# A graph layer's scatter-sum, hidden layer and normalization: batches turned in their own step, late x multiplied early, spans of 112 columns

## What is computed

```python
agg = segment_sum(edge_attr, dst, num_segments=6250)
h = concatenate([x, agg, u[batch]], axis=1)      # 128 + 128 + 16; batch is all zeros
h = relu(h @ W1 + b1)                            # 256 hidden
y = x + (h @ W2 + b2 + x)
out = (y - mean(y)) / sqrt(var(y) + 1e-5)        # over the 128 features
```

## Time and profile before

| | |
|---|---|
| Time, three runs | 185.32, 185.44, 185.79 us |
| The profiled execution: its time, its span | 185.73 us, 184.0 us |
| Granted clock of TensorE, mean | 0.994 of full speed (2.4 GHz) |
| Busy: TensorE, VectorE, ScalarE, GpSimd | 154.1, 115.4, 51.5, 25.4 us |
| DMA | 62.07 MB, mean 337 GB/s |
| HBM read and written | 58.50 MB, 3.20 MB |

### The profile page before, as it was taken

One profiled execution on the slowest core, in us unless ns is written; L12 is line 12 of the kernel. 1 busy time (PEld: TensorE's weight loads), 2 busy tenths in 40 slices (PEclk: granted clock), 3 DMA queues, 4 the chain that ended last, 5 costly groups with the idle time before them and its releaser, 6 DMA issues.

```text
span 184.0 us, 5378 instructions
## 1 busy us (share of the span) xinstructions
PE 154.1 (84%) x2195; PEld 113.9 (62%) x2195; DVE 115.4 (63%) x369; ACT 51.5 (28%) x110; POOL 25.4 (14%) x29
## 2 busy tenths in 40 slices
PE   0056979979979979969979999899889799899970
PEld 0046855955955956845846858467458568677850
DVE  6847499568376385485495466954933745877371
ACT  2021233223323313313313343133133241233230
POOL 7800030110200200200200204002003230000000
PEclk9999999999999999999999999999999999999997
DMA  5999999999999999999999999999999999998011
GB/s 119 315 352 373 374 375 373 371 373 374 374 374 373 375 372 373 376 372 373 374 373 374 375 373 374 375 373 360 363 374 374 371 374 370 367 398 303 11 43 33
DMA packets 42196, 62.07 MB, mean 337 GB/s; under 512 B 1975, under 2 KB 39541, under 8 KB 42170
## 3 DMA queue, kind: packets, MB, share of 16 engines
q1 hardware_dynamic: 41046, 61.23, 95.0%
q10 hardware_dynamic: 1124, 0.48, 1.2%
HBM read 58.50 MB, written 3.20 MB: 335 GB/s over the span
## 4 chain that ended last, share of the span: by engine, by line
PE 44%; DMA 39%; SPq 8%; DVE 4%; ACT 1%; issue 1%; DVEq 0%
DMA edge_ring<-in_edge_attr_dram 37%; PE sum_ps L845 17%; PE turn_ps L867 7%; PE hid_ps L907 6%; PE hid_ps L900 6%; PE out_ps L920 5%; SPq L276 4%; SPq L291 3%; DMA base_row<-in_dst_dram 2%; DVE bases L568 2%; PE xt_ps L920 1%; PE xt_ps L882 1%; DVE local_rows L576 1%; ACT local_t L429 1%; PE xt_ps L834 1%
## 5 line engine op out<-in xcount | busy, mean ns | idle before, releaser
L845 PE MATMUL sum_ps<-edge_ring,onehot 128*32 128x128 f32 x1662 | 58.5, 284 | 13.0 <-DMA edge_ring<-in_edge_attr_dram 10.8
L845 PEld LDWEIGHTS sum_ps<-edge_ring,onehot 128*32 128x32 f32 x1662 | 45.2, 113 | 27.9 <-DMA edge_ring<-in_edge_attr_dram 13.3
L630 DVE TENSOR_TENSOR agg_t<-agg_t,turn_ps 128x128 f32 x70 | 20.2, 288 | 56.7 <-PE turn_ps L867 52.6
L594 DVE TENSOR_TENSOR onehot<-iota,local_t 128x768 f32<-128x768 f32 (+1 forms) x40 | 33.6, 843 | 3.0 <-ACT local_t L429 2.4
L402 POOL TENSOR_TENSOR x_all<-x_all,half_b 128x512 f32<-128x512 f32 (+3 forms) x16 | 17.7, 1115 | 127.4 <-PE xt_ps L882 127.4
L466 ACT ACTIVATE hid_t<-hid_ps,bias 128x512 f32<-128x512 f32 (+3 forms) x32 | 18.1, 584 | 37.1 <-PE hid_ps L907 37.1
L867 PE MATMUL turn_ps<-place,sums 128*128 128x128 f32 (+1 forms) x140 | 26.5, 306 | 0.0
L907 PE MATMUL hid_ps<-agg_t,w_a 128*128 128x512 f32 (+3 forms) x64 | 24.1, 500 | 0.6 <-DVE agg_t L630 0.5
L867 PEld LDWEIGHTS turn_ps<-place,sums 128*128 128x128 f32 (+1 forms) x140 | 18.9, 192 | 8.0 <-issue 7.9
L920 PE MATMUL out_ps<-w_sb,hid_t 128*128 128x128 f32 (+1 forms) x176 | 21.9, 275 | 0.0
L441 ACT COPY sums<-sum_ps 128x256 f32<-128x256 f32 (+2 forms) x40 | 13.6, 341 | 25.9 <-PE sum_ps L845 25.9
(11 more groups left out here) (64 smaller groups left out, 73.0 us busy)
## 6 DMA issues: line engine op xcount, KB each, us to landing
edge_ring<-in_edge_attr_dram SPq DMA_DIRECT2D x69, 768.0 KB, 12.1
x_all<-in_x_dram SPq DMA_DIRECT2D x10, 256.0 KB, 10.5
out_dram<-x_all SPq DMA_DIRECT2D x1, 2304.0 KB
dst_rows<-in_dst_dram SPq DMA_DIRECT2D x1, 384.0 KB
x_all<-in_x_dram SPq DMA_DIRECT2D x1, 384.0 KB, 11.1
out_dram<-x_all SPq DMA_DIRECT2D x3, 128.0 KB
out_dram<-x_all SPq DMA_DIRECT2D x1, 256.0 KB
w_x<-in_L_gnn_W_dram ACTq DMA_DIRECT2D x1, 128.0 KB, 5.9
```

The lines of the kernel that those rows point to most:

```text
L594: nc.vector.tensor_tensor(onehot[0:ROWS, b % BUFFERS, 0:k * TILES], cols, loc, ALU.is_equal).then_inc(onehot_ready, 1)
L630: nc.vector.tensor_tensor(to, to, turn_ps[b % 2][:, i * SPAN:(i + 1) * SPAN], ALU.add).then_inc(group_added, 1)
L845: last = nc.tensor.matmul(bank[c * WIN:(c + 1) * WIN], onehot[0:p, b % BUFFERS, i * TILES + c * R + r], edge_ring[0:p, slot, c * R + r], s ...
```

## The change

Seven things are done together.

1. TensorE turns a batch in the step in which it sums it. Between the two it does hidden or output work, where there is any. There is one bank for sums and one for turns, and two banks `keep_ps` in their place. The turn waits for the additions of the batch before.
2. `SPAN` is 112 and no longer 128, in place, turn and addition.
3. Pairs go on to group 65; groups 66 to 69 are singles. The pieces at the end are A, B, C_ (256 each), ODD (106), E and END (128 each).
4. The late rows of x are loaded after groups 2, 3, 4, 5, 7 and 8, transposed in steps 3, 5 and 6, and multiplied by their half of W1 in steps 5 to 7 and 28. The products of A and B are copied out of PSUM (`x_hid_late`), and VectorE adds the aggregate halves to them (`add_x_hidden`); those of C_, ODD, E and END stay in PSUM, in keep_ps and xt_ps.
5. A 512 piece's x half is formed a step ahead of its aggregate half; its x is transposed at the end of a step, behind the turn.
6. VectorE adds a batch in its own step, ahead of the builds; onehot and place are made further ahead, in five buffers. What follows an output is spread over steps: residual addition, moments, scaling.
7. GpSimd does the scaling of LAST, A, B, C_ and ODD: 11 instructions.

The constants, pieces, steps and banks:

```diff
-SPAN = P
+SPAN = 112
...
-BUFFERS = 3
+BUFFERS = 5
+AHEAD = 5
...
+COMPLETE_AT = [6, 12, 18, 24, 30, 36, 40, 46, 52, 58, 60, 64, 66, 67, 68]
+SINGLE0 = 66
+LATE_LOAD_AT = [2, 3, 4, 5, 7, 8]
+LATE_TURN_STEP = [3, 5, 6]
+LATE_SUM_STEP = [5, 6, 7]
...
     pieces = [(b * BLOCK, P, J) for b in range(n_big)]
     pieces += [(late0 + h * half, P, J // 2) for h in range(3)]
-    pieces += [(rest0 - 2 * P, P, 1), (rest0 - P, P, 1), (rest0, rest_nodes, 1)]
+    pieces += [(odd0, odd_nodes, 1), (n_nodes - 2 * P, P, 1), (n_nodes - P, P, 1)]
...
-    complete_at = [6, 12, 18, 24, 30, 36, 40, 46, 52, 58, 60, 63, 66, 67, 69, n_grp]
+    complete_at = COMPLETE_AT + [n_grp]
...
-    single0 = 60
-    batch_first = list(range(0, single0, PAIR)) + list(range(single0, n_grp)) + [n_grp]
...
+    batch_first = list(range(0, SINGLE0, PAIR)) + list(range(SINGLE0, n_grp)) + [n_grp]
...
-    hidden_step = [batch_first.index(complete_at[n]) for n in range(n_big)]
-    out_step = [b + 1 for b in hidden_step]
-    turn_x_step = [1] + out_step[:n_big - 1]
...
-    x_parts = [(n,) for n in range(n_big)] + [(A, B), (C_, D, E), (REST,)]
-    x_load_at = {1: 0} | {IT * n: n for n in range(1, n_big)}
-    x_late_at = 53
...
+    hidden_step = [batch_first.index(c) for c in complete_at]
+    out_step = [min(h + 1, n_batch) for h in hidden_step]
+    y_step = out_step
+    moments_step = [o + (n < LAST) for n, o in enumerate(out_step)]
+    root_step = [m + 1 for m in moments_step]
+    scale_step = root_step
+    pool_scaled = range(LAST, E)
...
+    made_by = [min(b + 3 + sum(hidden_step[n] <= b for n in range(AHEAD - 2)), n_batch) for b in range(n_batch)]
...
+    late_parts = [(A, B), (C_, ODD), (E, END)]
+    turns = sorted([(1 if n == 0 else out_step[n - 1], (n,)) for n in range(n_big)]
+                   + list(zip(LATE_TURN_STEP, late_parts)))
...
+    hidden_x_step = [max(h - 1, turns[turned_at[n]][0] + 1) for n, h in enumerate(hidden_step[:n_big])]
...
-        sum_ps = [psum(f"sum_ps{i}", [P, BLOCK]) for i in range(2)]
-        turn_ps = [psum(f"turn_ps{i}", [P, BLOCK]) for i in range(2)]
...
+        sum_ps = psum("sum_ps", [P, BLOCK])
+        turn_ps = psum("turn_ps", [P, BLOCK])
+        keep_ps = [psum(f"keep_ps{m}", [P, BLOCK]) for m in range(m_chunks)]
```

The loads, GpSimd, VectorE and TensorE:

```diff
-                if g == x_late_at:
-                    load_x_late()
+                if g in LATE_LOAD_AT:
+                    load_x_late(LATE_LOAD_AT.index(g))
...
+            def scale_rows(n):
+                _, p, j = pieces[n]
+                pool.wait_ge(rstd_ready, n + 1)
+                for slot in range(x_slot[n], x_slot[n] + j):
+                    last = nc.gpsimd.tensor_scalar(x_all[0:p, slot], x_all[0:p, slot], mean_var[0:p, slot, 0:1],
+                                                   rstd[0:p, slot:slot + 1], ALU.subtract, ALU.mult)
+                last.then_inc(late_normalized, 1)
+            for b in range(scale_step[END] + 1):
+                for k, (turn_step, _) in enumerate(turns):
+                    if turn_step == b:
+                        add_half_b2(k)
+                for n in pool_scaled:
+                    if scale_step[n] == b:
+                        scale_rows(n)
...
+            def add_x_hidden(n):
+                dve.wait_ge(hidden_summed, m_chunks * (n + 1))
+                if n == A:
+                    dve.wait_ge(late_x_kept, m_chunks)
+                for m in range(m_chunks):
+                    xh = x_hid_late[:, m, late_cols(n)]
+                    nc.vector.tensor_tensor(xh, hidden_bank(n, m), xh, ALU.add).then_inc(late_added, 1)
...
+            for b in range(n_batch):
...
-                if b + 2 < n_batch:
-                    make_onehot(b + 2)
-                if b + 1 < n_batch:
-                    make_place(b + 1)
-                if b > 0:
-                    add_batch(b - 1)
...
+                for n in (A, B):
+                    if hidden_step[n] == b:
+                        add_x_hidden(n)
+                add_batch(b)
+                for m in range(made_by[b - 1] if b > 0 else 2, made_by[b]):
+                    make_onehot(m)
+                    make_place(m - 1)
+                if b == n_batch - AHEAD - 1:
+                    make_place(n_batch - 1)
...
-                    pe.wait_ge(group_added, batch_first[b - 1])
-                w = C * WIN if b < n_batch - 1 else WIN
+                if b > 0:
+                    pe.wait_ge(group_added, batch_first[b])
...
-                    last = nc.tensor.matmul(turn_ps[b % 2][:, i * SPAN:(i + 1) * SPAN], sums[0:w, b % 2, i],
+                    last = nc.tensor.matmul(turn_ps[:, i * SPAN:(i + 1) * SPAN], sums[0:w, b % 2, i],
                                             place[0:w, b % BUFFERS, i], start=True, stop=True)
...
+            def sum_x_kept():
+                pe.wait_ge(x_t_ready, turned_at[A] + 1)
+                for m in range(m_chunks):
+                    nc.tensor.matmul(keep_ps[m][:, 0:2 * half], w1_x[:, m * P:(m + 1) * P], x_t_late[:, part_cols(0)],
+                                     start=True, stop=True).then_inc(late_x_summed, 1)
+            def sum_x_late(n, m, clear):
+                nc.tensor.matmul(hidden_bank(n, m), w1_x[:, m * P:(m + 1) * P], x_t_late[:, late_cols(n)],
+                                 start=clear, stop=False, skip_group_check=True)
...
+                if A <= n <= B:
+                    pe.wait_ge(hidden_ready, m_chunks * n_big)
...
+                    pe.wait_ge(y_ready, n)
+                elif n in (B, E):
+                    pe.wait_ge(late_added, m_chunks * (1 if n == B else 2))
+                elif n > A:
+                    pe.wait_ge(y_ready, {C_: A, ODD: B, END: C_}[n] + 1)
...
-            late_step = batch_first.index(single0)
-            for b in range(late_step):
+            for b in range(n_batch):
                 sum_batch(b)
-                if b > 0:
-                    turn_batch(b - 1)
+                for n in range(n_pieces):
+                    if n < n_big and hidden_x_step[n] == b:
+                        sum_hidden_x(n)
+                    if hidden_step[n] == b:
+                        sum_hidden_a(n)
+                for n in range(END):
+                    if out_step[n] == b and n not in range(B, E):
+                        sum_out(n)
+                turn_batch(b)
+                for n in range(B, E):
+                    if out_step[n] == b:
+                        sum_out(n)
...
+                for k, (turn_step, _) in enumerate(turns):
+                    if turn_step == b:
+                        turn_x(k)
+                if LATE_SUM_STEP[0] == b:
+                    sum_x_kept()
+                if LATE_SUM_STEP[1] == b:
+                    pe.wait_ge(x_t_ready, turned_at[C_] + 1)
+                    pe.wait_ge(late_x_kept, 1)
+                    for m in range(m_chunks):
+                        sum_x_late(C_, m, m == 0)
+                if LATE_SUM_STEP[2] == b:
+                    pe.wait_ge(x_t_ready, turned_at[E] + 1)
+                    pe.wait_ge(late_x_kept, 2)
+                    sum_x_late(E, 0, True)
+                    sum_x_late(E, 1, False)
+                    sum_x_late(END, 1, False)
+                if b == last_x_step:
+                    pe.wait_ge(x_t_ready, len(turns))
+                    sum_x_late(ODD, 0, True)
+                    sum_x_late(ODD, 1, False)
+                    sum_x_late(END, 0, False)
+            sum_hidden_a(END)
+            sum_out(END)
```

More of the change, by code:

```diff
@@ L177, in hidden_bank, with late_cols, part_cols, hidden_out @@
                 return hid_ps[m][:]
-            return hid_ps[n % 2][:, m * half:m * half + p * j]
+            bank, at = {A: (hid_ps[0], 0), B: (hid_ps[1], 0), C_: (keep_ps[0], 0), ODD: (xt_ps, 0),
+                        E: (keep_ps[1], 0), END: ((xt_ps, 2 * P), (keep_ps[1], P))[m]}[n]
+            return bank[:, at + m * p * j:at + (m + 1) * p * j]
+        def late_cols(n):
+            node0, p, j = pieces[n]
+            return slice(node0 - late0, node0 - late0 + p * j)
+        def part_cols(k):
+            return slice(late_cols(late_parts[k][0]).start, late_cols(late_parts[k][-1]).stop)
+        def hidden_out(n, m):
+            _, p, j = pieces[n]
+            to = hid_t[:, n % 2, m] if n < n_big else hid_t_late[:, (n - n_big) % 3, m, 0:p * j]
+            return to
         def out_bank(n):
-            return xt_ps if n >= n_big and n % 2 == 0 else out_ps
+            return {B: hid_ps[0], ODD: hid_ps[0], E: hid_ps[1]}.get(n, out_ps)
         pad_set = sem("pad_set")
@@ L187, in gnn_resnorm_kernel @@
         edges_landed = [sem(f"edges_landed{i}") for i in range(SLOTS)]
-        x_landed = [sem(f"x_landed{k}") for k in range(len(x_parts))]
+        x_landed = [sem(f"x_landed{k}") for k in range(len(turns))]
         consts_ready = sem("consts_ready")
@@ L327, in store, with wait_scaled @@
                     sp.dma_start(to[cut:p], src[cut:p]).then_inc(stored, 16)
```

(33 more changed lines are left out.)

362 lines of the change are left out of this document (142 added, 220 removed).

## The result

| | before | after |
|---|---|---|
| Median of four runs each | 185.47 us (185.32 to 185.79) | 176.85 us (176.72 to 177.16) |
| Span of the profiled execution | 184.0 us | 175.4 us |
| Ratio of the times, 95% interval | | 0.9536 (0.9518 to 0.9553) |

A forecast was written before the change was run, and what follows sets the result against it. Loads set the pace first, then TensorE's backlog after 144.5 us; group 69 starting 6.2 us earlier and a shorter end cut the span by 8.1 to 175.9, and 175.9 + 1.73 - 0.29 gave 177.3 us, range 175.5 to 181.

The forecast's parts named there:

- the point where it turns: Late part: TensorE works off its backlog and meets the data at group 65, landing at 157.1 us.
- The sum for three batches: Middle: TensorE's work for three batches of two groups takes 11.9 us, against 13.3 for the DMA.
- 1.4 us to spare: Middle: TensorE's spare time per period of three batches, which makes good the late x by about 70 us.
- I take nothing: Hand-over between sum and turn: hidden or output work covers ScalarE's copy in nearly every pair; uncovered, 0.6 us each.
- rival 4: Bare hand-over in each batch makes the kernel slower; 0.6 us exposure costs the whole gain; chance 0.06.
- Rival 2: Cover between sum and turn is partial; each of the last 9 batches loses 0.35 us more: 180.4 us; chance 0.15.
- The 0.25 that I had added for uncovered copies: Late singles: uncovered copy time of 0.15 us at group 67 and 0.1 at group 68.
- So the loads run at one pace: Edge loads throughout: a steady 374 GB/s, 2.10 us per full group, stopping long before the end.
- group 59 at 144.5: Late x loaded early moves the same bytes by 144.5 us, so group 59 lands where it did.
- The late part: From group 65 to the sum of 69: 10.3 us, so group 69 starts at 167.4, 6.2 us earlier.
- The end: After the sum of 69 starts at 167.4: last scaling ends at 172.95, span at 175.9 us.
- The lock (rival 3): Port lock between VectorE and GpSimd: LAST's scalings delay builds and an addition, some 1.5 us on TensorE: 178.8; chance 0.08.

The follow-up runs named there:

- x_mid: Changed kernel with the late x loaded after groups 20 to 26 and turned and multiplied nine steps later, still in the middle: 177.00 us.
- x_late: Changed kernel with the late x loaded after groups 42 to 48 and its work twenty steps later: 179.29 us.
- edges_al: Changed kernel with two unused 128-byte pads, so that edge_ring and x_all both start on multiples of 256 bytes: 170.63 us, ratio 0.9193.
- the bare order: Changed kernel with each batch turned right behind its sum, hidden and output work behind the turn: four runs of 190.26 to 193.81 us.
- x_off128: Changed kernel with 128 unused bytes ahead of x_all, which then starts 128 bytes past a multiple of 256: 178.04 us.
- y_first_e: Changed kernel with residual additions of LAST and A ahead of their step's additions, and E's output behind the last turn: 176.33 us, ratio 0.9511.
- before_al: Kernel before with an unused 128-byte pad ahead of edge_ring, so edge_ring and x_all start on multiples of 256 bytes: 179.71 us, ratio 0.9688.

## Why the prediction was right, and where it was off

**What bounds the kernel.** Right in kind: first the loads set the pace, then TensorE's work. x_mid and x_late show the division: the same 4.2 us are free in the middle and cost 2.4 late. But the point where it turns was forecast at group 65, 157.1, and TensorE waited for edges last at 134.97, for group 55. The sum for three batches was right (11.9 forecast, 11.88 in edges_al). Yet "1.4 us to spare" does not hold in all nine periods: the one between the pieces complete at groups 36 and 40 has two batches, 9.81 us of TensorE against 9.1 of loads, 0.7 too much. Eight times 1.4 less 0.7 is 10.5, near the 10.8 of the earlier trace rows. Take from 10.8 the late x (4.2), the two copy waits (1.1) and the edges' lead (1.1), and 4.4 are left; after shows 4.2.

**The turn in its own step.** "I take nothing": right. Without cover it costs 0.50 in each of 37 batches and turns the sign, which was rival 4. Its price was wrong: by its own sum an exposure of 0.50 would cost 28 x 0.03 + 9 x 0.5 = 5.3 us and give some 182.6, and the bare order took 190.3 at least. It gave the middle some 0.47 us to spare in each of 28 batches, 13 us, where 4.2 were left. Rival 2, partial cover of every late batch, did not come: two copy waits, in the first two steps. The 0.25 that I had added for uncovered copies were absent.

**"So the loads run at one pace", group 59 at 144.5.** This is the term that was mis-sized. The pace was taken to belong to the queue and the bytes; part of it belonged to where x_all lies. Loads of x had slowed the queue, and with x_all on a multiple of 256 bytes the edges came 1.1 us earlier. x_off128 takes that away: 178.04 us, and the sum of 69 at 167.77 where 167.4 was forecast. So for the kernel that I had reasoned about I was 0.7 too low, and the address gave 1.2 back: that 177.3 lies only 0.5 from the 176.85 measured is partly luck.

**The late part.** From the meeting to the sum of 69: 10.3 forecast, 10.3 measured. The wait of 0.3 for VectorE's additions is there with 0.39. The wait of 0.67 for the output bank was missed. It fell between groups 59 and 65, where 11.4 us of work had been set against 12.6 of data; measured are 12.3 from the second half of pair 58/59 to that of 64/65, the wait included. Only some 0.2 of it counted: y_first_e took it away, and TensorE then waited 0.44 for group 65. That wait, and the 10.3 from its landing (155.56) to the sum of 69 (165.85), are what the forecast had described. The narrow span was worth 0.4 us by the medians, within the noise (forecast 0.05 for a pair and 0.03 for a single, 0.37 for the five pairs and four singles behind 135). The pairs up to 65 were worth 2.3 us, of which the forecast had named 1.1 together with the span, and none of the hand-overs.

**The end.** Sum of 69 to the end of the last scaling: 5.55 forecast, 6.03 measured (166.50 to 172.53 in the chain). The 0.48 are waits that I had priced as signals only: 0.46 for the last addition and 0.58 for the ReLU. From there to the end of the span 2.95 forecast, 2.87 measured. So 177.3 - 0.90 (sum of 69 earlier) + 0.48 - 0.08 = 176.8.

**The lock (rival 3).** Its cause was there, its price was not. Onehot took 1213 ns and not 944, 8.9 us of VectorE over 33 pairs, and GpSimd's scaling 0.80 and not 0.45. The cause of the first is where GpSimd's instructions fall (1.62 us beside one, 0.95 without), not that it has more of them (952 ns in the bare order, with the same 34.3 us). But TensorE waits for no onehot in the middle of the program in after: five buffers and builds five batches ahead take it. What may remain of it is the residual addition of LAST, late behind a onehot. A version with the scalings on VectorE wasn't tried, so that share stays open.

**What no run isolates.** Of the seven parts, the late x was moved and the pairs and the span were undone one at a time, and the cover of part 1 was taken away. What turning a batch in its own step brings by itself, and parts 5, 6 and 7, were not measured alone; before_al speaks for part 6 (additions first), without proving it.

## What to carry to other kernels

Find the place where the engine that is late meets the loads: work ahead of it is free up to the spare time that the waits for loads show (use those waits, 10.8 us in the kernel before, and not a spare time per period times the number of periods), and work behind it counts in full. A hand-over to another engine may stand in every batch if work of its length stands inside it; without that, 0.5 us per batch were worth more than the whole change. And when a kernel is bound by loads, look at the byte at which their targets start in a partition, in the kernel before and after every change of a tile's size.

## What the runs showed of the hardware

**A load's pace depends on where its target starts in the partition.** Loads of edges (1536 bytes in a row of a partition) ran at 374 GB/s with edge_ring 128 bytes past a multiple of 256, and at 398 with it on one: 6.4% more, for 128 unused bytes. It took after from 176.85 to 170.63 us and before, where x_all moved to a multiple with it, from 185.72 to 179.71. The blocks of x show it too: in after every third slice or so of the middle, up to the 26th, stands at 380 to 384; in x_off128 none from the fifth to the 36th is above 377. Only these two places were tried, so whether 64 or 32 bytes past cost as much is open.

The Trainium skill (DMA: Bandwidth & Descriptors, section "How a descriptor splits into AXI transactions") says that a transfer is cut at multiples of 256 bytes, and that the first piece of one that starts between them begins at the multiple below, part of it unused; it says so of what is read. An estimate from it: a row of 1536 bytes that starts 128 past needs 52 beats of 32 bytes in place of 48, 8.3% more. The runs, 6.4%, agree in kind, and show it for the side that is written.

The same page (section "Where 436 GB/s comes from") has about 358 GB/s as what binds a core's loads from HBM. The measurement decides against it for one core working alone: 398 GB/s in the stretches above.

**A wait hidden behind loads is not gone.** In the kernel before, 0.5 us of waits for the additions showed; with faster loads 5.6 did.
